# Attention on one NeuronCore: in each half unit the scores for the maximum are sent ahead of the scores for the exponentials

## The chip, the core and the metric

The kernel runs on one core of one Trainium2 chip. A core has five engines that run side by side, each through its own list of instructions in order, and that meet only at semaphores: TensorE (PE in the profile; PEld is its weight load), VectorE (DVE), ScalarE (ACT), GpSimd (POOL) and SyncE (SP, which here only starts DMAs). TensorE writes its results into PSUM, a small memory of 8 banks; VectorE and ScalarE read them there. The metric is the device time of one execution in microseconds (us), the median of the runs.

## What is computed

A "macaron" block on x of 16 x 512 x 128: half a feed-forward layer, an attention layer, half a feed-forward layer, each with a layer norm and a residual. The change touches the attention alone:

```
HEADS, HEAD_DIM = 16, 8
q = (x @ Wq.T + bq).reshape(b, s, HEADS, HEAD_DIM)     # k, v alike
attn = einsum('bqhd,bkhd->bhqk', q, k) / sqrt(HEAD_DIM)
attn = softmax(attn, axis=-1) * head_mask
out = einsum('bhqk,bkhd->bqhd', attn, v) @ Wo.T + bo

x = x + 0.5 * ffn(layernorm(x))      # stage ffn1
x = x + attention(layernorm(x))      # stage attention
x = x + 0.5 * ffn(layernorm(x))      # stage ffn2
```

## The kernel before

The program runs a setup, `ffn1`, `attention` and `ffn2` one after the other. The attention takes 16 batches of 512 rows. The 16 heads are four groups of four, and the 512 positions are four tiles of 128, so that a batch has 16 **units** (a group and a tile), and a unit has two **halves**, of two heads each.

Each score is computed twice. The softmax needs the maximum of each query's scores before the exponentials. So the kernel first computes the scores with the queries on the partitions (`score_max`, L1114; below **max scores**), and VectorE reduces them to the negated maximum (`take_max`, L1372, the reduction on L1379). The maxima of a group are split into two parts on GpSimd (`split_max`), turned on TensorE (`turn_max`), copied on ScalarE (`copy_max`) and packed by DMA into rows of the `q_pack` operand (`pack_max`). The scores that are computed a second time with the keys on the partitions (`score_exp`, L1100; below **exp scores**) then come out with the maximum already taken off, and ScalarE takes their exponentials (`exponential`, L1246, the activation on L1249). The exponentials are multiplied with the values (`times_values`, L1128), accumulated over the four tiles of a group in the bank `p_o`. The max scores run `AHEAD` = 8 units, that is 16 halves, ahead of the exp scores.

A half of either kind of scores is two 32-row by 128-column matmuls with 512 moving columns; the two write the two banks of one **score buffer**. Half 0 of the exp scores uses the array's row strips 0 and 1 and half 1 strips 2 and 3; `HALVES` gives the max scores the other two strips in the same half, so that both kinds can run in the array side by side.

There are three score buffers `p_score` (6 of the 8 banks), and both kinds of scores take them in turn: `order` (L1042 to L1048) lists all halves as they are sent, `place` numbers them, and `score_bank` takes the buffer `place % 3`. `bank_free` (L1055) makes a score wait until the entry three places before it in `order` has been read: by VectorE (semaphore `max_read`) if that is a max score, by ScalarE (`exp_ready`) if it is an exp score.

TensorE's list is written out by hand in `batch` (L1173). Per unit: half 0 sends exp scores, max scores, then one **piece** at most (`pieces`, L1193: a transposition, a projection, all through the one bank `p_x`, whose users wait for each other through `x_bank_filled` and `x_bank_drained`); half 1 sends exp scores, max scores, then `times_values` of the unit before. ScalarE's list is one exponential per half and between them small copies; VectorE's is one reduction per half and between them the statistics of a later layer norm (units 2 and 3), `normalise` (units 2, 6, 10, 14), `residual` (unit 4) and `copy_values` (unit 7). The scores of a group need the packed maxima: before each fourth unit TensorE waits for `max_packed`.

Of the kernel before, what the change touches and what calls it, by code (L numbers as in the profile page):

```python
# [29 lines left out]
NT = S // P  # L30
# [5 lines left out]
NQ = HEADS // QUAD  # L36
# [942 lines left out]
def attention(nc, w, front, src, dst):  # L979
# [6 lines left out]
    MAX_DMA = MAX_PARTS * 16  # L986
    MAX_SPLIT = MAX_PARTS
    inv_sqrt = 1.0 / HD ** 0.5
    with ExitStack() as ctx:
# [25 lines left out]
        max_packed = pair(sem, "max_packed")  # L1015
# [7 lines left out]
        def there(b, n=0):  # L1023

            return not isinstance(b.j, int) or b.k + n < NB
# [16 lines left out]
        order = [("max", 0, n) for n in range(2 * AHEAD)]  # L1042
        for k in range(NB):
            for n in range(PAIRS):
                order.append(("exp", k, n))
                ahead = k * PAIRS + n + 2 * AHEAD
                if ahead < NB * PAIRS:
                    order.append(("max", ahead // PAIRS, ahead % PAIRS))  # L1048
        place = {pair_of_scores: at for at, pair_of_scores in enumerate(order)}

        def score_bank(kind, b, n):

            return p_score[place[kind, b.k, n] % len(p_score)]

        def bank_free(pe, kind, b, n):  # L1055

            at = place[kind, b.k, n] - len(p_score)
            if at >= 0:
                before, k, m = order[at]
                pe.wait_ge({"max": max_read, "exp": exp_ready}[before], k * PAIRS + m + 1)  # L1060
# [36 lines left out]
        def _(pe):  # L1097


            def score_exp(b, u, half):  # L1100

                g, t = divmod(u, NT)
                n = 2 * u + half
                bank_free(pe, "exp", b, n)
                for i in range(2):
                    j = 2 * half + i
                    rows = slice(j * ROWS, (j + 1) * ROWS)
                    last = nc.tensor.matmul(score_bank("exp", b, n)[:, i, :],  # L1108
                                            pack["k"][b.par][rows, g, t * P:(t + 1) * P],
                                            pack["q"][b.par][rows, g, :], start=True, stop=True,  # L1110
                                            tile_position=(j * ROWS, 0))
                last.then_inc(exp_tile, 1)

            def score_max(b, u, half):  # L1114


                g, t = divmod(u, NT)
                n = 2 * u + half
                bank_free(pe, "max", b, n)
                for j in HALVES[half]:  # L1120
                    rows = slice(j * ROWS, (j + 1) * ROWS)
                    last = nc.tensor.matmul(score_bank("max", b, n)[:, j % 2, :],  # L1122
                                            pack["q"][b.par][rows, g, t * P:(t + 1) * P],
                                            pack["k"][b.par][rows, g, :], start=True, stop=True,
                                            tile_position=(j * ROWS, 0))
                last.then_inc(max_tile, 1)

            def times_values(b, u):  # L1128

                g, t = divmod(u, NT)  # L1130
                pe.wait_ge(exp_ready, b.count(PAIRS, 2 * (u + 1)))
                if t == 0:
                    need(pe, o_copied, b.count(NQ, g))
                if u == 0:
                    first_batch = isinstance(b.j, int) and b.k == 0
                    pe.wait_ge(x_bank_drained, FIRST_USES.index("v") + 1 if first_batch
                               else uses(b.step(-1), "v") + 1)
                for h in range(QUAD):
                    last = nc.tensor.matmul(p_o[h * COLS:(h + 1) * COLS, :],  # L1139
                                            values[b.par][:, t, g * QUAD + h, :],  # L1140
                                            exps[(2 * u + h // 2) % len(exps)][:, h % 2, :], start=t == 0, stop=t == NT - 1,
                                            tile_position=(0, h * COLS))
                last.then_inc(pv_done, 1)
# [29 lines left out]
            def batch(b, is_first, is_last):  # L1173
                a, c = b.step(-1), b.step(1)
                for u in range(UNITS):
                    if u % NT == 0:
                        g = u // NT
                        pe.wait_ge(max_packed[g % 2], b.count(MAX_DMA * NQ // 2, MAX_DMA * (g // 2 + 1)))
                    ahead, v = (b, u + AHEAD) if u + AHEAD < UNITS else (c, u + AHEAD - UNITS)
                    if v == 0 and there(ahead):  # L1180
                        pe.wait_ge(packed[ahead.par], ahead.half(PACK_DMA, PACK_DMA))
                    for half in range(2):
                        score_exp(b, u, half)
                        if there(ahead):
                            score_max(ahead, v, half)
                        if half == 0:
                            pieces(b, u, is_first)
                        elif u > 0:
                            times_values(b, u - 1)
                        elif not is_first:  # L1190
                            times_values(a, UNITS - 1)

            def pieces(b, u, is_first):  # L1193
                a, c, e = b.step(-1), b.step(1), b.step(2)
                if u == 1:
                    turn_max(b, 1, uses(b, "m1"))
                if not is_first:
                    if u == 2:
                        turn_o(a, 3, uses(b, "o3"))
                    if u == 3:  # L1200
                        turn_norm(uses(b, "norm"))
                    if u == 4:
                        project_out(uses(b, "out"))
                if u == 5:
                    turn_max(b, 2, uses(b, "m2"))
                if u == 6:
                    turn_o(b, 0, uses(b, "o0"))
                if u == 7 and there(c):
                    front.project_v(pe, p_x, uses(b, "v"))
                if u == 8 and there(e):  # L1210
                    front.turn_x(pe, p_x, e, uses(b, "x"))
                if u == 9:
                    turn_max(b, 3, uses(b, "m3"))
                if u == 10:
                    turn_o(b, 1, uses(b, "o1"))
                if u == 11 and there(e):
                    front.project_qk(pe, p_x, e, w.wq, uses(b, "q"))
                if u == 12 and there(e):
                    front.project_qk(pe, p_x, e, w.wk, uses(b, "k"))
                if u == 13 and there(c):  # L1220
                    turn_max(c, 0, uses(b, "m0"))
                if u == 14:
                    turn_o(b, 2, uses(b, "o2"))
# [292 lines left out]
```

## Time and profile before

| | us |
|---|---|
| time, median of 3 runs | 2008.73 (2007.45 to 2009.02) |
| the profiled execution: its own time | 2005.38 |
| the profiled execution: span from first to last instruction | 2003.2 |
| TensorE busy over the span | 1792.4 (89%) |
| VectorE busy | 1494.7 (75%) |
| ScalarE busy | 1231.5 (61%) |
| GpSimd busy | 891.7 (45%) |

The profile is one execution on the chip. A row of the timeline gives when instructions started, how long they were busy, and in square brackets how long their engine had been idle before and whose work ended that. The attention stage lies between about 602 and 1420 us of the span. Its first scores are sent before 604.26 us, its regular rhythm runs from about 620 us on, and in the last eight units of the last batch no max scores are left to send. TensorE's granted clock is a share of full speed: 1.00 is 2.4 GHz and 0.50 is 1.2 GHz.

### The profile page before, as it was taken

How to read it: one execution, taken by the hardware profiler on the slowest of the kernel's cores; microseconds unless marked ns; L12 is line 12 of the kernel's file. 1: busy time of each engine (PE TensorE's matmuls, PEld its weight loads, DVE VectorE, ACT ScalarE, POOL GpSimd, SP SyncE). 2: the span in 40 equal slices, each digit the busy share in tenths (PEclk: the TensorE clock that was granted, in tenths of full speed). 3: DMA queues.
4: the chain of work that ended last, by engine and by line, in shares of the span. 5: the costliest groups of instructions: out<-in, count | busy, mean ns of one | idle time of the engine just before them, and what ended most of it. 6: DMA issues, size and time to landing. Idle time of an engine off the chain costs nothing. (4 is left out here: it accounts for less than half of the span.)

```text
span 2003.2 us, 30167 instructions
## 1 busy us (share of the span) xinstructions
PE 1792.4 (89%) x9569; PEld 1090.6 (54%) x9600; DVE 1494.7 (75%) x2379; ACT 1231.5 (61%) x1914; POOL 891.7 (45%) x878
## 2 busy tenths in 40 slices
PE   3999999999887888888888888888589999999999
PEld 2777777777662333333333333333267777777777
DVE  4768776877747888888888888888168776877775
ACT  3565555555453777777777777777455556555554
POOL 3665566555661222222222222221145556555655
PEclk9999999999995999999999999999789999999999
DMA  3001000000011111111111111110100000000000
GB/s 95 22 11 32 22 31 10 31 21 19 24 49 45 51 51 51 51 51 51 51 51 51 51 51 51 46 46 13 37 1 33 22 32 11 31 21 30 12 21 11
DMA packets 42269, 69.59 MB, mean 35 GB/s; under 512 B 8508, under 2 KB 10036, under 8 KB 42164
## 3 DMA queue, kind: packets, MB, share of 16 engines
q1 hardware_dynamic: 37360, 66.20, 10.0%
q0 software_dynamic: 4096, 1.08, 0.3%
q8 instruction: 58, 0.95, 0.2%
q10 hardware_dynamic: 708, 0.98, 0.1%
q14 instruction: 47, 0.39, 0.1%
HBM read 28.36 MB, written 12.58 MB: 20 GB/s over the span
## 5 line engine op out<-in xcount | busy, mean ns | idle before, releaser
L762 POOL TENSOR_TENSOR ffn_hid_low<-ffn_hidden,ffn_hid_high 128x512 fp32r<-128x512 f32 x448 | 581.1, 1299 | 457.5 <-ACT ffn_hid_high L674 456.9
L1379 DVE TENSOR_REDUCE attn_neg_max<-attn_p_score 128x2 f32<-128x1024 f32 x512 | 623.5, 1223 | 125.5 <-PE attn_p_score L1122 123.3
L1249 ACT ACTIVATE attn_exps<-attn_p_score 128x1024 f32<-128x1024 f32 x512 | 520.1, 1025 | 219.5 <-PE attn_p_score L1108 217.4
L674 ACT ACTIVATE ffn_hid_high<-ffn_hidden 128x512 fp32r<-128x512 f32 x448 | 281.2, 628 | 257.5 <-DVE ffn_hidden L923 256.0
L665 ACT ACTIVATE ffn_silu<-ffn_p_gate 128x512 f32<-128x512 f32 x448 | 264.3, 590 | 212.8 <-PE ffn_p_gate L518 212.6
L916 DVE TENSOR_TENSOR ffn_gated<-ffn_silu,ffn_p_up 128x512 f32<-128x512 f32 x352 | 240.6, 684 | 181.7 <-PE ffn_p_up L518 118.2
L1122 PE MATMUL attn_p_score<-k_pack,q_pack 32*128 32x512 f32 x1024 | 262.1, 511 | 52.4 <-ACT attn_exps L1249 36.2
L1139 PE MATMUL attn_p_o<-attn_exps,values 128*32 128x512 f32 x2048 | 278.8, 616 | 8.4 <-ACT attn_o_raw L1255 3.4
L1108 PE MATMUL attn_p_score<-q_pack,k_pack 32*128 32x512 f32 x1024 | 253.3, 504 | 1.1 <-DVE attn_neg_max L1379 1.1
L923 DVE TENSOR_TENSOR ffn_hidden<-ffn_gated,ffn_p_spread 128x512 f32<-128x512 f32 x352 | 240.9, 684 | 14.7 <-remote 4.1
L1108 PEld LDWEIGHTS attn_p_score<-q_pack,k_pack 32*128 32x128 f32 x1024 | 95.1, 185 | 266.0 <-issue 235.1
L516 PE MATMUL ffn_p_y<-ffn_hid_high,down_high 128*128 128x512 f32 x448 | 186.5, 416 | 33.6 <-POOL ffn_hid_low L762 32.8
L516 PE MATMUL ffn_p_gate<-ffn_xt_high,gate_high 128*128 128x512 f32 x448 | 189.0, 422 | 0.0
L516 PE MATMUL ffn_p_up<-ffn_xt_high,up_high 128*128 128x512 f32 x448 | 180.9, 404 | 3.1 <-DVE ffn_gated L916 2.9
L1326 POOL DMA_DIRECT2D q_pack<-attn_max_rows x128 | 74.3, 582 | 243.2 <-ACT attn_max_rows L1243 243.2
L518 PE MATMUL ffn_p_gate<-ffn_xt_low,gate_high 128*128 128x512 f32 x448 | 177.6, 397 | 0.0
L518 PE MATMUL ffn_p_up<-ffn_xt_low,up_high 128*128 128x512 f32 x448 | 177.2, 396 | 0.0
L518 PE MATMUL ffn_p_y<-ffn_hid_low,down_high 128*128 128x512 f32 x448 | 177.2, 396 | 0.0
L517 PE MATMUL ffn_p_up<-ffn_xt_high,up_low 128*128 128x512 f32 x448 | 177.1, 395 | 0.0
L517 PE MATMUL ffn_p_gate<-ffn_xt_high,gate_low 128*128 128x512 f32 x448 | 177.0, 395 | 0.0
L517 PE MATMUL ffn_p_y<-ffn_hid_high,down_low 128*128 128x512 f32 x448 | 175.8, 392 | 0.0
L1122 PEld LDWEIGHTS attn_p_score<-k_pack,q_pack 32*128 32x128 f32 x1024 | 96.6, 187 | 107.9 <-ACT attn_exps L1249 91.5
(168 smaller groups left out, 2182.3 us busy)
## 6 DMA issues: line engine op xcount, KB each, us to landing
q_pack<-attn_q_high SPq DMA_DIRECT2D x32, 256.0 KB
k_pack<-attn_k_high SPq DMA_DIRECT2D x32, 256.0 KB
ffn_x_in<-in_x SPq DMA_DIRECT2D x16, 256.0 KB, 2.8
ffn_x_res<-in_x SPq DMA_DIRECT2D x16, 256.0 KB, 3.2
after_ffn<-ffn_x_out SPq DMA_DIRECT2D x16, 256.0 KB, 2.1
attn_x_in<-after_ffn SPq DMA_DIRECT2D x16, 256.0 KB, 2.8
k_pack<-attn_k_low SPq DMA_DIRECT2D x16, 256.0 KB
q_pack<-attn_q_low SPq DMA_DIRECT2D x16, 256.0 KB
```

What stands on the lines that cost most here:

```text
L516: nc.tensor.matmul(out, weights[0], high, start=start, stop=False)
L517: nc.tensor.matmul(out, weights[1], high, start=False, stop=False)
L518: return nc.tensor.matmul(out, weights[0], low, start=False, stop=stop)
L665: nc.scalar.activation(silu[f % 2][0:n, :], p_gate[f % 2][0:n, :], ACT.Silu).then_inc(silu_ready, 1)
L674: nc.scalar.activation(hid_high[s][0:n, :], hidden[s][0:n, :], ACT.Copy).then_inc(high_ready, 1)
L762: nc.gpsimd.tensor_tensor(hid_low[s][0:n, :], hidden[s][0:n, :], hid_high[s][0:n, :].bitcast(F32), ALU.subtract).then_inc(low_ready, 1)
L923: V.tensor_tensor(hidden[slot(b, f)][:], gated[f % 2][:], p_spread[:], ALU.mult).then_inc(weighted_ready, 1)
L1108: last = nc.tensor.matmul(score_bank("exp", b, n)[:, i, :], pack["k"][b.par][rows, g, t * P:(t + 1) * P], pack["q"][b.par][rows, g, :], st ...
L1122: last = nc.tensor.matmul(score_bank("max", b, n)[:, j % 2, :], pack["q"][b.par][rows, g, t * P:(t + 1) * P], pack["k"][b.par][rows, g, :] ...
L1139: last = nc.tensor.matmul(p_o[h * COLS:(h + 1) * COLS, :], values[b.par][:, t, g * QUAD + h, :], exps[(2 * u + h // 2) % len(exps)][:, h % ...
L1249: nc.scalar.activation(exps[n % len(exps)][:], score_bank("exp", b, n)[:], ACT.Exp, scale=inv_sqrt)\
L1379: V.tensor_reduce(neg_max[g % 2][:, j:j + 2, t], score_bank("max", b, n)[:], AX.X, ALU.max, negate=True).then_inc(max_read, 1)
```

## The change

In each half the max scores are sent before the exp scores. `order` is turned in the same way, so that the buffers and the waits follow. With this the entry three places before a max score is the exp score of two halves before, and the entry three places before an exp score is the max score of the half before. Until now it was the exp score of the half before for a max score, and the max score of two halves before for an exp score. The wait for `max_packed`, which stood ahead of a unit's scores, moves into `score_exp`, behind the first max scores of the unit.

```diff
--- before.py
+++ after.py
@@ -1042,10 +1042,10 @@
         order = [("max", 0, n) for n in range(2 * AHEAD)]
         for k in range(NB):
             for n in range(PAIRS):
-                order.append(("exp", k, n))
                 ahead = k * PAIRS + n + 2 * AHEAD
                 if ahead < NB * PAIRS:
                     order.append(("max", ahead // PAIRS, ahead % PAIRS))
+                order.append(("exp", k, n))
         place = {pair_of_scores: at for at, pair_of_scores in enumerate(order)}
 
         def score_bank(kind, b, n):
@@ -1101,6 +1101,8 @@
 
                 g, t = divmod(u, NT)
                 n = 2 * u + half
+                if t == 0 and half == 0:
+                    pe.wait_ge(max_packed[g % 2], b.count(MAX_DMA * NQ // 2, MAX_DMA * (g // 2 + 1)))
                 bank_free(pe, "exp", b, n)
                 for i in range(2):
                     j = 2 * half + i
@@ -1173,16 +1175,13 @@
             def batch(b, is_first, is_last):
                 a, c = b.step(-1), b.step(1)
                 for u in range(UNITS):
-                    if u % NT == 0:
-                        g = u // NT
-                        pe.wait_ge(max_packed[g % 2], b.count(MAX_DMA * NQ // 2, MAX_DMA * (g // 2 + 1)))
                     ahead, v = (b, u + AHEAD) if u + AHEAD < UNITS else (c, u + AHEAD - UNITS)
                     if v == 0 and there(ahead):
                         pe.wait_ge(packed[ahead.par], ahead.half(PACK_DMA, PACK_DMA))
                     for half in range(2):
-                        score_exp(b, u, half)
                         if there(ahead):
                             score_max(ahead, v, half)
+                        score_exp(b, u, half)
                         if half == 0:
                             pieces(b, u, is_first)
                         elif u > 0:
```

TensorE's list in unit 15 of a batch, a unit without a piece, before (rows of L1108 are exp scores, of L1122 max scores; each half is two rows; `attn_p_score0` to `2` are the three buffers, `attn_max_read` is VectorE's semaphore and `attn_exp_ready` ScalarE's; the last row is the first of `times_values`):

```order
L1108 MATMUL attn_p_score0<-q_pack0,k_pack0 128x512 [waits attn_max_read]
L1108 MATMUL attn_p_score0<-q_pack0,k_pack0 128x512
L1122 MATMUL attn_p_score1<-k_pack1,q_pack1 128x512 [waits attn_exp_ready]
L1122 MATMUL attn_p_score1<-k_pack1,q_pack1 128x512
L1108 MATMUL attn_p_score2<-q_pack0,k_pack0 128x512 [waits attn_max_read]
L1108 MATMUL attn_p_score2<-q_pack0,k_pack0 128x512
L1122 MATMUL attn_p_score0<-k_pack1,q_pack1 128x512 [waits attn_exp_ready]
L1122 MATMUL attn_p_score0<-k_pack1,q_pack1 128x512
L1139 MATMUL attn_p_o<-attn_exps4,values0 32x512 [waits attn_exp_ready]
```

The same place now (L1124 are max scores, L1110 exp scores):

```order
L1124 MATMUL attn_p_score0<-k_pack1,q_pack1 128x512 [waits attn_exp_ready]
L1124 MATMUL attn_p_score0<-k_pack1,q_pack1 128x512
L1110 MATMUL attn_p_score1<-q_pack0,k_pack0 128x512 [waits attn_max_read]
L1110 MATMUL attn_p_score1<-q_pack0,k_pack0 128x512
L1124 MATMUL attn_p_score2<-k_pack1,q_pack1 128x512 [waits attn_exp_ready]
L1124 MATMUL attn_p_score2<-k_pack1,q_pack1 128x512
L1110 MATMUL attn_p_score0<-q_pack0,k_pack0 128x512 [waits attn_max_read]
L1110 MATMUL attn_p_score0<-q_pack0,k_pack0 128x512
L1141 MATMUL attn_p_o<-attn_exps4,values0 32x512 [waits attn_exp_ready]
```

The second half's exp scores now stand directly ahead of `times_values` and take the buffer of the first half's max scores, sent three places before; until now the second half's max scores stood there and took the buffer of the first half's exp scores.

Unit 12, which begins a group and has the projection of k (L337 to L339) as its piece, before:

```order
L1108 MATMUL attn_p_score0<-q_pack0,k_pack0 128x512 [waits attn_max_read,attn_max_packed1]
L1108 MATMUL attn_p_score0<-q_pack0,k_pack0 128x512
L1122 MATMUL attn_p_score1<-k_pack1,q_pack1 128x512 [waits attn_exp_ready]
L1122 MATMUL attn_p_score1<-k_pack1,q_pack1 128x512
L337 MATMUL attn_p_x<-attn_xt_high,wk_high 128x512 [waits attn_x_bank_drained,attn_xt_low_ready]
L338 MATMUL attn_p_x<-attn_xt_high,wk_low 128x512
L339 MATMUL attn_p_x<-attn_xt_low,wk_high 128x512
L1108 MATMUL attn_p_score2<-q_pack0,k_pack0 128x512 [waits attn_max_read]
```

and now:

```order
L1124 MATMUL attn_p_score0<-k_pack1,q_pack1 128x512 [waits attn_exp_ready]
L1124 MATMUL attn_p_score0<-k_pack1,q_pack1 128x512
L1110 MATMUL attn_p_score1<-q_pack0,k_pack0 128x512 [waits attn_max_read,attn_max_packed1]
L1110 MATMUL attn_p_score1<-q_pack0,k_pack0 128x512
L337 MATMUL attn_p_x<-attn_xt_high,wk_high 128x512 [waits attn_x_bank_drained,attn_xt_low_ready]
L338 MATMUL attn_p_x<-attn_xt_high,wk_low 128x512
L339 MATMUL attn_p_x<-attn_xt_low,wk_high 128x512
L1124 MATMUL attn_p_score2<-k_pack1,q_pack1 128x512 [waits attn_exp_ready]
```

The wait for the packed maxima (`attn_max_packed1`) now has the unit's first max scores ahead of it. The lists of VectorE, ScalarE, GpSimd and SyncE hold the same operations in the same order as before.

## Rows read from the trace of the kernel before

**Rows 1.** By stretch: length, engines' busy us (count), granted TensorE clock, DMA share, GB/s

```profile
620.00:644.00 24.00, 21.54 (x90) 5.69 (x90) 15.38 (x23) 11.59 (x14) 7.27 (x11) 0.50 0.01 2
644.00:1400.00 756.00, 670.99 (x4592) 260.38 (x4588) 641.78 (x774) 563.38 (x701) 208.11 (x336) 1.00 0.15 47
```

**Rows 2.** Waits between 644 and 1400 us: who <- for whom, us, times, longest

```profile
ACT attn_exps L1249 <- PE attn_p_score L1108: 192.4, 258, 1.9
DVE attn_neg_max L1379 <- PE attn_p_score L1122: 110.2, 322, 1.4
PEld attn_p_score L1122 <- ACT attn_exps L1249: 85.2, 139, 1.0
...
PEld attn_p_score L1108 <- DVE attn_neg_max L1379: 6.5, 32, 0.2
```

**Rows 3.** Timeline of TensorE, units 15 and 0: start, busy, what

```profile
1074.05 1.06 PE L1139 MATMUL attn_p_o<-attn_exps,values 128*32 128x512 f32 x8
1075.04 0.50 PE L1108 MATMUL attn_p_score<-q_pack,k_pack 32*128 32x512 f32 x2
1075.05 0.50 PE L1122 MATMUL attn_p_score<-k_pack,q_pack 32*128 32x512 f32 x2
1075.43 0.50 PE L1108 MATMUL attn_p_score<-q_pack,k_pack 32*128 32x512 f32 x2
1076.66 0.50 PE L1122 MATMUL attn_p_score<-k_pack,q_pack 32*128 32x512 f32 x2 [0.72 <-ACT attn_exps L1249]
1077.09 1.07 PE L1139 MATMUL attn_p_o<-attn_exps,values 128*32 128x512 f32 x8
1078.09 0.50 PE L1108 MATMUL attn_p_score<-q_pack,k_pack 32*128 32x512 f32 x2
```

**Rows 4.** Timeline of ScalarE, the same units

```profile
1075.58 1.94 ACT L1249 ACTIVATE attn_exps<-attn_p_score 128x1024 f32<-128x1024 f32 x2 [0.59 <-PE attn_p_score L1108]
```

**Rows 5.** Timeline of VectorE, the same units

```profile
1074.15 1.23 DVE L1379 TENSOR_REDUCE attn_neg_max<-attn_p_score 128x2 f32<-128x1024 f32 x1 [0.35 <-PE attn_p_score L1122]
...
1077.20 1.23 DVE L1379 TENSOR_REDUCE attn_neg_max<-attn_p_score 128x2 f32<-128x1024 f32 x1 [0.20 <-PE attn_p_score L1122]
```

**Rows 6.** Timeline of TensorE: one piece per batch, in two batches running

```profile
1040.85 1.16 PE L1169 MATMUL attn_p_x<-wo,attn_ot 128*128 128x128 f32 x8
...
1088.54 0.66 PE L1163 MATMUL attn_p_x<-ident,attn_o_norm 128*128 128x128 f32 x4 [0.71 <-DVE attn_o_norm L1393]
...
1091.23 1.16 PE L1169 MATMUL attn_p_x<-wo,attn_ot 128*128 128x128 f32 x8
1092.32 0.50 PE L1108 MATMUL attn_p_score<-q_pack,k_pack 32*128 32x512 f32 x2
```

**Rows 7.** Timeline of VectorE, units 2 to 4

```profile
1086.01 0.86 DVE L262 BATCH_NORM_STATS2 attn_stats<-attn_x_in 128x6 f32<-128x128 f32 x4
1086.78 1.21 DVE L1379 TENSOR_REDUCE attn_neg_max<-attn_p_score 128x2 f32<-128x1024 f32 x1
1087.91 0.25 DVE L1390 RECIPROCAL attn_sums_inv<-attn_p_x 128x16 f32<-128x16 f32 x1
...
1088.40 1.22 DVE L1379 TENSOR_REDUCE attn_neg_max<-attn_p_score 128x2 f32<-128x1024 f32 x1
1089.53 0.15 DVE L269 TENSOR_TENSOR attn_mean_sum<-attn_stats 128x4 f32<-128x4 f32 x1
...
1090.29 2.35 DVE L1379 TENSOR_REDUCE attn_neg_max<-attn_p_score 128x2 f32<-128x1024 f32 x2
...
1094.04 0.68 DVE L1400 TENSOR_TENSOR attn_x_out<-attn_p_x,attn_x_bias 128x512 f32<-128x512 f32 x1
1094.64 2.50 DVE L1379 TENSOR_REDUCE attn_neg_max<-attn_p_score 128x2 f32<-128x1024 f32 x2
```

**Rows 8.** Timeline of TensorE, two units while the granted clock is 0.50

```profile
625.36 0.79 PE L1108 MATMUL attn_p_score<-q_pack,k_pack 32*128 32x512 f32 x2
...
629.86 0.79 PE L1108 MATMUL attn_p_score<-q_pack,k_pack 32*128 32x512 f32 x2
```

## The prediction

> **What bounds the kernel now.** I read the busy time by stretch first. Between 644 and 1400 us, where the attention runs in its regular rhythm, TensorE is busy for 671.0 of 756 us, VectorE for 641.8 and ScalarE for 563.4 [rows 1]. That is 89%, 85% and 75%: nobody is full. The waits come next. ScalarE waits 192.4 us for exp scores, VectorE 110.2 us for max scores, and on TensorE's side 139 weight loads of max scores waited for an exponential, 85.2 us in all, while the exp scores waited only 6.5 us for VectorE's reductions, never over 0.2 us at a time [rows 2]. So the stage is a ring of waits, and the timeline shows which.
>
> Take unit 15, which has no piece. Its first exp scores start at 1075.04 [rows 3]; ScalarE starts on them at 1075.58, 0.54 us later [rows 4]; the second half's max scores, which want that buffer, start at 1076.66, 1.08 us after the exponential's start; `times_values` follows at 1077.09, 0.43 us on; the next unit's exp scores start at 1078.09, 1.00 us later [rows 3]. Sum: 0.54 + 1.08 + 0.43 + 1.00 = 3.05 us, the unit's period. The link through ScalarE's exponential is one of four. VectorE's reductions are a branch beside the ring.
>
> One piece (the output projection) comes back after 1091.23 - 1040.85 = 50.38 us [rows 6]. So a batch takes 50.38 us, against 16 x 3.05 = 48.80. The other 1.58 us are units whose piece waits. The worst that I show: the transposition L1163 waits 0.71 us for VectorE's `normalise` [rows 6].
>
> **The change part by part.** No instruction is added or removed, only TensorE's order and the buffers change. 16 batches x 16 units, less the 8 last units, where no max scores are left, are 248 units, or 15.5 batches, that feel it.
>
> *The new ring.* After `times_values` TensorE sends the first half's max scores, then exp scores, then the second half's max scores, and then exp scores that want the buffer of the first half's max scores. They wait for VectorE's reduction, and `times_values` and everything of the next unit are queued behind them. The links:
> - max scores to the start of their reduction: 0.54 us (1076.66 to 1077.20) [rows 3, 5];
> - start of a reduction to the scores that want its buffer: 1.28 us. The trace shows it once in this unit: reduction at 1074.15, exp scores at 1075.43 [rows 3, 5]. It fits the reduction's 1.23 us;
> - scores to `times_values` 0.43, and that to the next scores 1.00 us, as before.
>
> Sum: 0.54 + 1.28 + 0.43 + 1.00 = **3.25 us** per unit, 0.20 more than now: the exponential's 1.08 is replaced by the reduction's 1.28. 248 x 0.20 = **+49.6 us**.
>
> *The other new waits.* Lay a unit off from its first max scores at 0. The reduction starts at 0.54, the next, queued behind it, at 1.68 (1.14 us from one VectorE start to the next: 1086.78 to 1087.91 is 1.13 [rows 7]), and ends its claim on the buffer at 2.96. The next unit's first exp scores want it at 3.25. 0.29 us of room: no cost. The max scores now want the exponential of two halves before. The second half's exp scores start at 1.82, their exponential at 2.36, the buffer is free at 3.44, and it is wanted by the next unit's second max scores at 3.25 + 0.39 = 3.64. Room 0.20, and a copy of ScalarE between the halves stands behind the exponential, not ahead of it. No cost. The wait for the packed maxima is passed later than before by one pair of scores, and it does not show among the waits now [rows 2]; no cost. SyncE's and GpSimd's DMAs are where they were.
>
> *What VectorE does between its reductions* was beside the ring and is now in it. The statistics (unit 2) take 0.77 us from start to next start (1086.01 to 1086.78), `normalise` 0.49 (1087.91 to 1088.40), the variance steps of unit 3 0.76 (1089.53 to 1090.29), `residual` 0.60 (1094.04 to 1094.64) [rows 7]. I lay units 2 to 5 off in the ring:
> - Unit 2, first max scores at 0. Reductions at 0.54 and, after the statistics, at 2.45 instead of 1.68. `normalise` follows, and VectorE is free at 2.45 + 1.14 + 0.49 = 4.08. Unit 3's max scores are there at 3.25, so that their reduction would have started at 3.79: **+0.29**.
> - Unit 3: reductions at 4.08 and, after the variance steps, at 4.08 + 1.14 + 0.76 = 5.98. Unit 4's first exp scores wait until 5.98 + 1.28 = 7.26, and the projection behind them takes to 7.26 + 0.43 + 1.09 = 8.78 (1091.23 to 1092.32 [rows 6]). Unit 4's second exp scores so start at 8.78; by the ring they would be at 4.08 + 1.28 + 3.25 = 8.61: **+0.17**.
> - Unit 4: the second reduction starts at 9.32, `residual` at 10.46, VectorE is free at 11.06. Unit 5's max scores came at 8.78 + 1.43 = 10.21 and would have been taken at 10.75: **+0.31**.
>
> Sum 0.77 us per batch. The other `normalise` and `copy_values` fall into VectorE's new pause behind the second reduction, from 1.68 + 1.14 = 2.82 to 3.79, so 0.97 us wide, and cost nothing. The pieces' waits that make the 1.58 us of now go: the second max scores are sent at about 0.4 instead of 1.6 us into the unit, so the reduction before `normalise` starts at 1.68 instead of 1.62 + 0.54 = 2.16, and what waited is ready when its turn comes. The pieces themselves (1.09 us at most) fit under 1.82. So a batch has 16 x 3.25 + 0.77 = 52.77 us instead of 50.38, **+2.39**; 15.5 x 2.39 = **+37.0 us**.
>
> At the 0.50 clock the unit is 4.50 us (625.36 to 629.86 [rows 8]), with the same exponential in it, so that the 0.20 holds there too.
>
> Bounds of what the trace doesn't show: with no extra at all in a batch, 15.5 x (16 x 3.25 - 50.38) = +25.1; with the 1.58 us of now staying and nothing new, +49.6; with 0.77 on top, +61.5. I take 37.0, since each wait was laid off by itself.
>
> What a reader costs is also in the notes. By the Trainium skill (Perfetto Trace Analysis, Optimizing Scalar/DVE Operations) an access to PSUM costs VectorE about 125 ns beyond the elements and ScalarE about 51 ns, and with the clocks of Trainium Kernel Development and Optimization, NeuronCore Architecture (0.96 and 1.2 GHz) 1024 elements give an estimate of 1.19 and 0.90 us, 0.29 apart. The trace shows the two from start to next user 1.28 and 1.08, 0.20 apart. By the page's 0.29 the first term would be 71 us instead of 49.6, and the time about 2067; I go by the trace.
>
> **Level.** The profiled execution took 2005.38 us with a span of 2003.2. The new span: 2003.2 + 37.0 = 2040.2. On the median of 2008.73: **2045.7 us**.
>
> **The rivals.**
> *Faster: VectorE is fed sooner.* VectorE is the busier of the two readers and its 110.2 us of waiting are for the very scores that are now sent first [rows 2]. If its earlier start shortened the ring, the 1.58 us per batch would be won and nothing paid: -15.5 x 1.58 = -24.5, so 1984. It decides if the new link through the reduction is no longer than the old one, that is if max scores at TensorE are released within 0.54 + 1.08 = 1.62 us; the row gives 1.82. Against it: the first max scores of a unit cannot be sent before `times_values`, which stands behind the wait for the last ones, so VectorE only trades a pause in mid-unit for one of 0.97 us at its end.
> *No change.* The gain on the pieces offsets the ring: with 1.58 us gone and nothing new, this needs a ring only 0.10 us longer, so a release 1.18 us after the reduction's start. The row has 1.28 and the reduction alone is busy for 1.23. About 2009.
> *The clock falls.* TensorE stands still within each unit from the second max scores to the exp scores, 0.5 + 0.4 to 1.82, 0.9 us instead of 0.72 now [rows 3]. At 0.50 a unit takes 4.50 against 3.05 [rows 3, 8], so each unit there costs 1.45 us. A stage wholly at 0.50 would take 240 x 1.45 = 348 us more, about 2390; a later rise at the start by five units 7 us. For it: the clock was at 0.50 from 620 to 644 us although TensorE was busy 21.5 of 24 us [rows 1]. Against it: it then stayed at 1.00 through 756 us with a standstill of 0.72 us in each unit.
> The Trainium skill (Perfetto Trace Analysis, Matmul Optimizations) says that TensorE's power scales with its use and that matmuls should be sent back to back; by it this rival is the one to fear, while the trace so far shows the full clock with pauses.
>
> **How the numbers follow.** The forecast, a longer ring with between +25 and +61 us, holds 0.88; faster by the first rival 0.04; no change 0.04; the clock 0.04. The range of 2032 to 2064 runs from the lower bound (2033.8) to a little over 2058, the case of the old waits staying, and most of the way to the upper one (2070). A measurement of this kernel can tell about 0.2% from no change, 4 us. Faster by more than that 0.04, within it 0.04, slower 0.92.
>
> **What would show it.** The output projection comes back after 52.8 us instead of 50.38. In unit 15 the second half's exp scores start 1.82 us after the first max scores and wait for VectorE, the max scores wait for nobody, and TensorE's waits for exponentials (85.2 us) turn into waits for reductions of some 0.9 us per unit, over 200 us in all. ScalarE and VectorE still wait, VectorE now ahead of each unit's first reduction. Units 3, 4 and 5 are longer than 3.25 us by 0.29, 0.17 and 0.31, and the others are not. Wrong if units of 3.05 us are left, if L1163 still waits 0.7 us, or if the granted clock is below 1.00 after 650 us.

## The result and the profile after

| | before | changed |
|---|---|---|
| median, us | 2008.09 (4 runs, 2006.14 to 2009.02) | 2059.41 (4 runs, 2058.55 to 2059.99) |
| profiled execution: its time / its span, us | 2005.38 / 2003.2 | 2059.99 / 2057.8 |
| mean granted TensorE clock | 0.978 | 0.969 |

The ratio is 1.0257, with a 95% interval of 1.0239 to 1.0274: the change makes the kernel slower by 51.3 us.

The ring is read first. The timeline of TensorE in the changed kernel, the last unit of one batch and the first of the next, answers to [rows 3] (L1124 max scores, L1110 exp scores, L1141 `times_values`):

```profile
1110.85 0.49 PE L1124 MATMUL attn_p_score<-k_pack,q_pack 32*128 32x512 f32 x2
1110.85 0.50 PE L1110 MATMUL attn_p_score<-q_pack,k_pack 32*128 32x512 f32 x2
1111.19 0.40 PE L1124 MATMUL attn_p_score<-k_pack,q_pack 32*128 32x512 f32 x2
1112.66 0.50 PE L1110 MATMUL attn_p_score<-q_pack,k_pack 32*128 32x512 f32 x2 [1.07 <-DVE attn_neg_max L1378]
1113.09 1.06 PE L1141 MATMUL attn_p_o<-attn_exps,values 128*32 128x512 f32 x8
1114.09 0.50 PE L1124 MATMUL attn_p_score<-k_pack,q_pack 32*128 32x512 f32 x2
```

and VectorE's row of the same unit, two reductions one behind the other:

```profile
1111.38 2.36 DVE L1378 TENSOR_REDUCE attn_neg_max<-attn_p_score 128x2 f32<-128x1024 f32 x2 [0.40 <-PE attn_p_score L1124]
```

The max scores of the first half start at 1110.85, their reduction at 1111.38 (0.53 later), the exp scores that want the buffer at 1112.66 (1.28 later), `times_values` at 1113.09 (0.43 later), the next unit at 1114.09 (1.00 later). Sum 3.24; forecast 0.54 + 1.28 + 0.43 + 1.00 = 3.25, before 3.05. The max scores of the second half go out at 1111.19, right behind the first ones, and then TensorE stands still for 1.07 us, on VectorE.

The waits in the same stage, between 644 and 1456 us, answer to [rows 2]:

```profile
ACT attn_exps L1248 <- PE attn_p_score L1110: 226.4, 426, 1.7
...
DVE attn_neg_max L1378 <- PE attn_p_score L1124: 169.8, 235, 2.3
PEld attn_p_score L1110 <- DVE attn_neg_max L1378: 149.4, 220, 1.5
PE attn_p_score L1110 <- DVE attn_neg_max L1378: 79.0, 154, 1.1
```

TensorE's weight loads waited 85.2 us for exponentials before; now they wait 149.4 us for reductions. VectorE, whose scores are now sent first, waits longer, not less: 169.8 instead of 110.2 us. Its waits are fewer (235 instead of 322); in the unit above the one wait stands before the first reduction (0.40 us), and the second reduction follows without one.

The output projection, once per batch, answers to [rows 6]:

```profile
1071.62 1.16 PE L1171 MATMUL attn_p_x<-wo,attn_ot 128*128 128x128 f32 x8
...
1128.35 1.16 PE L1171 MATMUL attn_p_x<-wo,attn_ot 128*128 128x128 f32 x8
...
1181.47 1.16 PE L1171 MATMUL attn_p_x<-wo,attn_ot 128*128 128x128 f32 x8
```

A batch now takes 1181.47 - 1128.35 = 53.12 us, and so do the batches around it, against 50.38. The one before it took 56.73. The view by stretch, with the granted clock before the DMA share, tells why, and answers to [rows 1] (length, busy us of TensorE, its weight loads, VectorE, ScalarE and GpSimd, clock, DMA share, GB/s):

```profile
602.00:662.00 60.00, 47.51 (x198) 16.51 (x198) 44.02 (x50) 23.29 (x27) 9.70 (x18) 0.57 0.12 41
702.00:707.00 5.00, 5.00 (x32) 2.00 (x24) 2.73 (x5) 2.74 (x4) 1.20 (x2) 0.68 0.10 37
752.00:762.00 10.00, 9.47 (x53) 3.24 (x49) 6.99 (x8) 5.76 (x7) 2.98 (x6) 0.72 0.18 57
1072.00:1090.00 18.00, 17.18 (x92) 7.28 (x91) 12.05 (x14) 9.58 (x11) 4.38 (x9) 0.72 0.09 31
1090.00:1456.00 366.00, 318.63 (x2104) 121.18 (x2102) 289.70 (x346) 266.28 (x321) 91.42 (x150) 1.00 0.13 42
```

The clock, at 1.00 throughout the rhythm before, falls to 0.50 three times, for 3 to 10 us each (about 702 to 705, 756 to 763 and 1077 to 1087 us); below these are the **dips**, and at the start of the stage it rises at about 654 us instead of about 644.

The span is 54.6 us longer. By the projection's periods:
- 15.5 batches x (53.12 - 50.38) = **42.5 us**, the ring and what is in it;
- the three batches with a dip took 54.25, 55.48 and 56.73 us, together **7.1 us** more than three of 53.12;
- the first projection comes 85.11 us after the first transposition of the maxima instead of 78.91, 6.2 us more, of which the ring in 20 units explains 3.4 (20/16 x 2.74): the later rise takes about **2.8 us**;
- that first transposition itself is 1.85 us later than before. The rest is 0.3 us.

That the later rise makes up the whole of the 2.8 us is not shown.

### The profile page after: what moved, and what is told of

It is laid out like the page before. It is cut to its first block and busy times, and to the rows that moved or that the text cites. A ratio compares the mean times of both kernels' runs of the same rounds, so it can differ in the third digit from the quotient of the medians.

```text
span 2057.8 us, 30213 instructions
## 1 busy us (share of the span) xinstructions
PE 1836.1 (89%) x9600; PEld 1105.1 (54%) x9600; DVE 1487.6 (72%) x2379; ACT 1249.6 (61%) x1914; POOL 892.1 (43%) x878
## 3 DMA queue, kind: packets, MB, share of 16 engines
q0 software_dynamic: 4096, 1.08, 0.3%
## 5 line engine op out<-in xcount | busy, mean ns | idle before, releaser
L1378 DVE TENSOR_REDUCE attn_neg_max<-attn_p_score 128x2 f32<-128x1024 f32 x512 | 612.0, 1222 | 184.3 <-PE attn_p_score L1124 180.7
L1110 PE MATMUL attn_p_score<-q_pack,k_pack 32*128 32x512 f32 x1024 | 261.2, 510 | 85.7 <-DVE attn_neg_max L1378 83.5
L1141 PE MATMUL attn_p_o<-attn_exps,values 128*32 128x512 f32 x2048 | 283.2, 625 | 6.9 <-ACT attn_o_raw L1254 5.9
L1124 PE MATMUL attn_p_score<-k_pack,q_pack 32*128 32x512 f32 x1024 | 254.9, 509 | 8.4 <-DVE attn_neg_max L1378 5.1
L1124 PEld LDWEIGHTS attn_p_score<-k_pack,q_pack 32*128 32x128 f32 x1024 | 97.7, 190 | 268.3 <-issue 211.5
L1110 PEld LDWEIGHTS attn_p_score<-q_pack,k_pack 32*128 32x128 f32 x1024 | 97.1, 186 | 175.9 <-DVE attn_neg_max L1378 157.2
```

Of the source, the lines that this page charges most:

```text
L1110: last = nc.tensor.matmul(score_bank("exp", b, n)[:, i, :], pack["k"][b.par][rows, g, t * P:(t + 1) * P], pack["q"][b.par][rows, g, :], st ...
L1141: last = nc.tensor.matmul(p_o[h * COLS:(h + 1) * COLS, :], values[b.par][:, t, g * QUAD + h, :], exps[(2 * u + h // 2) % len(exps)][:, h % ...
L1378: V.tensor_reduce(neg_max[g % 2][:, j:j + 2, t], score_bank("max", b, n)[:], AX.X, ALU.max, negate=True).then_inc(max_read, 1)
```

## The experiments

The theory: the ring of waits through the buffer that the first scores after `times_values` fill sets the unit's length. The rivals: VectorE or ScalarE bounds the stage in either order; what counts is only which kind of scores stands ahead of `times_values`; the moved wait for the packed maxima; the clock. All ratios are to the kernel before in the same comparison, and the batch is the period of the output projection at the full clock.

### Either reader made shorter, in both orders

```diff
-  V.tensor_reduce(neg_max[...], score_bank("max", b, n)[:], AX.X, ...)
+  V.tensor_reduce(neg_max[...], score_bank("max", b, n)[:, :, 0:416], AX.X, ...)
```

> The changed kernel, with each maximum taken over 416 of its 512 keys; the other keys are left out of the maximum (the softmax is the same with any offset near it). A reduction has 832 instead of 1024 elements and should be some 0.20 us shorter. Theory (the ring goes through VectorE's reduction): a unit goes from 3.25 to 3.05 us, 248 units give 50 us back, and if the dips of TensorE's clock inside the attention come from the longer standstills they go too: 2059 becomes about 2000 to 2010. Rival (VectorE is beside the ring and the loss is the clock or something of TensorE's own): a unit stays at 3.25 us and the time at about 2059.

> The kernel before, with the same shorter maximum over 416 of 512 keys. Theory: the reduction is a branch beside the ring, a unit stays at 3.05 us; only the pieces' waits for VectorE shrink, by at most 1.58 us per batch, so between 1984 and 2008. Rival (VectorE bounds both orders): 40 to 50 us faster here too, about 1960.

```diff
-  nc.scalar.activation(exps[...][:], score_bank("exp", b, n)[:], ACT.Exp, scale=inv_sqrt)
+  cols = slice(0, S if b.k == 0 else 416)
+  nc.scalar.activation(exps[...][:, :, cols], score_bank("exp", b, n)[:, :, cols], ACT.Exp, scale=inv_sqrt)
```

> The changed kernel, with the exponentials of 416 of 512 queries in all batches but the first; the exponentials of the other queries are left out there. An exponential should be some 0.16 us shorter. Theory: ScalarE is now beside the ring, a unit stays at 3.25 us and the time within 6 us of 2059; the cost of 0.25 us in unit 13, where the multiplication with the values waits for a copy of ScalarE, goes: up to 4 us. Rival (ScalarE still in the ring): 35 us faster, about 2024.

> The kernel before, with the same shorter exponentials (416 of 512 queries, the others are left out from the second batch on). Theory: the exponential is in the ring, 232 units lose 0.16 us each, 37 us faster, about 1971. Rival (VectorE bounds): no change, about 2008.

The groups between 800 and 1400 us (busy, mean ns of one) of the changed kernel with the short reduction, and then of the kernel before with the short exponential, show the sizes:

```profile
L1378 DVE TENSOR_REDUCE attn_neg_max<-attn_p_score 128x2 f32<-128x832 f32 x384 | 388.2, 1024 | 164.7 <-PE attn_p_score L1124 163.4 <-POOL attn_max_parts L1318 0.6
```

```profile
L1250 ACT ACTIVATE attn_exps<-attn_p_score 128x832 f32<-128x832 f32 x399 | 341.2, 864 | 190.8 <-PE attn_p_score L1108 188.6
```

A reduction is 0.20 us shorter (1.22 to 1.02), an exponential 0.16 us (1.02 to 0.86).

| | median, us | ratio to before (95%) | batch, us |
|---|---|---|---|
| changed order, short reduction | 2001.81 | 0.9973 (0.9963 to 0.9982) | 50.23 |
| old order, short reduction | 1994.51 | 0.9941 (0.9921 to 0.9961) | 49.64 |
| changed order, short exponential | 2052.19 | 1.0224 (1.0179 to 1.0269) | 52.83 |
| old order, short exponential | 1974.24 | 0.9840 (0.9813 to 0.9867) | 48.54 |

0.20 us off the reduction is worth 2.89 us per batch in the changed order (53.12 to 50.23) and 0.74 in the old one; 0.16 us off the exponential 1.83 in the old order and 0.29 in the changed one, where `times_values` no longer waits for ScalarE's copy in unit 13 (below). So the reader in the ring is VectorE after the change and ScalarE before it. With the short reduction the unit of the changed kernel reads 3.05 us from max scores to max scores, with its standstill at 0.88 instead of 1.07:

```profile
1021.54 0.50 PE L1124 MATMUL attn_p_score<-k_pack,q_pack 32*128 32x512 f32 x2
...
1023.16 0.50 PE L1110 MATMUL attn_p_score<-q_pack,k_pack 32*128 32x512 f32 x2 [0.88 <-DVE attn_neg_max L1378]
...
1024.59 0.50 PE L1124 MATMUL attn_p_score<-k_pack,q_pack 32*128 32x512 f32 x2
```

These four rule out that one and the same reader bounds the stage in both orders.

### The order turned in one half only

```diff
+  maxima = [("max", ahead // PAIRS, ahead % PAIRS)] if ahead < NB * PAIRS else []
+  order.extend(maxima + [("exp", k, n)] if n % 2 == H else [("exp", k, n)] + maxima)
...
+  if half != H: score_exp(b, u, half)
   if there(ahead): score_max(ahead, v, half)
+  if half == H: score_exp(b, u, half)
```

> The changed kernel, but the max scores go first in half 0 only; in half 1 the exp scores go first, as before the change, so that max scores stand ahead of the multiplication with the values. Theory: they take the buffer of the max scores of half 0, so the ring goes through the reduction: 3.25 us per unit, about 2050 to 2060. Rival (what counts is that exp scores stand ahead of the values): 3.05 us per unit, about 2008.

> The reverse: the max scores go first in half 1 only. The exp scores of half 1, ahead of the multiplication with the values, now take the buffer of the exp scores of half 0. Theory: the ring goes through the exponential, 3.05 us per unit, and the time is near 2008 (2000 to 2020). Rival (exp scores ahead of the values cost the time, whichever buffer they take): about 2059.

Max scores first in half 0 only: 2092.29 us, ratio 1.0415 (1.0391 to 1.0440), batch 53.42 at the full clock. Max scores first in half 1 only: 2012.02 us, ratio 1.0029 (1.0019 to 1.0039), batch 50.82. In the first the scores ahead of `times_values` are max scores, as before the change, and the ring is the longer one all the same, since their buffer comes from a reduction; in the second they are exp scores, as after it, and the ring is the short one:

```profile
1028.67 0.50 PE L1109 MATMUL attn_p_score<-q_pack,k_pack 32*128 32x512 f32 x2
1028.68 0.73 PE L1123 MATMUL attn_p_score<-k_pack,q_pack 32*128 32x512 f32 x4
1030.29 0.50 PE L1109 MATMUL attn_p_score<-q_pack,k_pack 32*128 32x512 f32 x2 [0.88 <-ACT attn_exps L1250]
1030.72 1.07 PE L1140 MATMUL attn_p_o<-attn_exps,values 128*32 128x512 f32 x8
1031.71 0.50 PE L1109 MATMUL attn_p_score<-q_pack,k_pack 32*128 32x512 f32 x2
```

(max scores first in half 1, TensorE; L1109 are exp scores: 3.04 us, with the wait for ScalarE.) In these four orders what counts is the kind of scores sent first after `times_values`. Where the second kernel's other 0.44 us per batch (50.82 against 50.38) come from was not followed up. The first of the two was 32 us above the top of its forecast, 2050 to 2060: its clock in the stage was 0.92, as its stretch from 644 us on shows:

```profile
644.00:1480.00 836.00, 725.79 (x4545) 272.62 (x4547) 638.10 (x769) 560.57 (x694) 206.71 (x333) 0.92 0.13 42
```

### The moved wait alone

```diff
   for u in range(UNITS):
+      if u % NT == 0: pe.wait_ge(max_packed[g % 2], ...)      # back in its old place
       ...
   def score_exp(b, u, half):
-      if t == 0 and half == 0: pe.wait_ge(max_packed[g % 2], ...)
```

> The changed kernel with the wait for the packed maxima back in its old place, ahead of the unit's first max scores. Theory: the packed maxima are there long before either place; the time is that of the changed kernel, 2059, within 3 us. Rival (the moved wait is part of the loss): more than 4 us faster.

2057.83 us, ratio 1.0259 (1.0240 to 1.0279), batch 53.02 against 53.12. The wait's place is worth 0.1 us a batch at most; the loss is the order's.

### The same ring length in the old order

```diff
   need(act, pv_done, ...)
+  nc.scalar.activation(spare[:, n % len(exps), :], w.ident[0:32, :], ACT.Copy)
   nc.scalar.activation(exps[n % len(exps)][:], ...)
```

> The kernel before with a small activation (a copy of 32x128) on ScalarE behind the wait for the exp scores, ahead of each exponential, so that the link through ScalarE is longer by that copy, 0.15 to 0.25 us, and the ring about as long as in the changed kernel, with the old order. Theory of the clock (TensorE's longer standstill in each unit makes the granted clock fall now and then): stretches at 0.50 inside the attention appear here too, and the time is that of the ring (248 x 0.2 = 50 us) and some 10 us more, 2055 to 2075. Rival (the dips belong to the changed order): the clock holds 1.00 from its rise to the end of the attention, and the time is 2045 to 2058.

2052.57 us, ratio 1.0221 (1.0201 to 1.0241), batch 52.79. TensorE's unit:

```profile
1050.36 0.50 PE L1109 MATMUL attn_p_score<-q_pack,k_pack 32*128 32x512 f32 x2
...
1052.17 0.50 PE L1123 MATMUL attn_p_score<-k_pack,q_pack 32*128 32x512 f32 x2 [0.91 <-ACT attn_exps L1251]
...
1053.60 0.50 PE L1109 MATMUL attn_p_score<-q_pack,k_pack 32*128 32x512 f32 x2
```

3.24 us, the length of the changed kernel's unit, made in the old order by 0.2 us in ScalarE's link. It costs 2.41 us per batch; the change costs 2.74. Its clock held 1.00 from the rise to the end of the rhythm (a stretch of 786 us has 0.99, its first microseconds below). So a longer ring with a standstill of 0.91 us does not by itself bring the dips.

### ScalarE's copy ahead of the multiplication in unit 13

The changed kernel's unit 13 is 3.50 us, not 3.25. TensorE and, below, ScalarE:

```profile
1105.92 0.50 PE L1110 MATMUL attn_p_score<-q_pack,k_pack 32*128 32x512 f32 x2 [0.26 <-DVE attn_neg_max L1378]
1106.60 1.06 PE L1141 MATMUL attn_p_o<-attn_exps,values 128*32 128x512 f32 x8 [0.18 <-ACT attn_o_raw L1254]
```

```profile
1104.14 0.68 ACT L360 ACTIVATE attn_k_full<-attn_p_x,bk 128x512 f32<-128x512 f32 x1
1104.94 1.02 ACT L1248 ACTIVATE attn_exps<-attn_p_score 128x1024 f32<-128x1024 f32 x1
1105.86 0.59 ACT L1254 ACTIVATE attn_o_raw<-attn_p_o 128x512 f32<-128x512 f32 x1
```

`times_values` starts 0.68 us after the scores instead of 0.43, since the copy of the last group's sums (L1254) stands behind an exponential whose scores had waited for VectorE. The copy moved up by half a unit:

```diff
-  if now == (13, 0):
+  if now == (12, 1):          # ahead of the copy of k
       copy_o(b, 2, uses(b, "o0") + 1)
```

> The changed kernel with ScalarE's copy of the third group's output sums moved ahead of the copy of k (half 1 of unit 12 instead of half 0 of unit 13). Theory: the 0.25 us per batch that the multiplication in unit 13 waits for that copy go, 15 x 0.25 = 4 us faster than 2059, if the later copy of k does not make the next transposition late by more than its room. Rival: the copy of k comes 0.5 us later, TensorE waits for it in unit 13, and the time is the same or worse.

The batch goes from 53.12 to 52.86 us, by the 0.25 us that the wait was long. (A transposition now waits up to 0.7 us for the later copy of k, the rival's mechanism, but within the time in which the exp scores behind it would have waited for VectorE.) The median did not follow: 2059.37 us, ratio 1.0258 (1.0230 to 1.0285), with single runs from 2044.16 to 2060.33. The profiled execution is the shortest (2044.16 us, mean granted clock 0.978, with one short dip); the other four took 2058.88 to 2060.33 at 0.966 or 0.967. So the clock differs between executions of one kernel, here along with some 15 us.

### The multiplication moved between the two scores of half 1

```diff
   score_exp(b, u, half)
+  if half == 1: times_values(b, u - 1)
   if there(ahead): score_max(ahead, v, half)
-  ... times_values(b, u - 1)
```

> The kernel before with the multiplication with the values of half 1 between that half's exp scores and its max scores, instead of behind both. Theory: the max scores wait 1.08 us for the exponential's end, and the multiplication takes 1.00 us of that; TensorE's ring is gone and a unit is bounded by what VectorE (2 x 1.14 us and its other work, 2.3 us per unit plus 4.6 us per batch) or TensorE does: 2.4 to 2.8 us per unit instead of 3.15, so 90 to 180 us faster, 1830 to 1920. Rival (the ring is not what bounds): no change, about 2008.

> The changed kernel with the multiplication with the values between the max scores and the exp scores of half 1. Theory: the wait for the reduction is covered in the same way, and both orders come out within 1% of each other, 1830 to 1930. Rival: the order itself costs its 50 us whatever covers the wait, so that it stays 2% to 3% slower than the one above.

Both forecasts were far off. The first took 2267.15 us (its runs from 2230.03 to 2277.62, so that even the shortest is 11% above the kernel before), the second 2411.45 us, ratio 1.2021 (1.1974 to 1.2067). Three things failed. First, the wait was not covered but handed on. TensorE in the first of them, at the full clock:

```profile
893.05 0.70 PE L1122 MATMUL attn_p_score<-k_pack,q_pack 32*128 32x512 f32 x4
893.39 0.40 PE L1108 MATMUL attn_p_score<-q_pack,k_pack 32*128 32x512 f32 x2
894.88 0.50 PE L1108 MATMUL attn_p_score<-q_pack,k_pack 32*128 32x512 f32 x2 [1.09 <-DVE attn_neg_max L1380]
895.31 1.07 PE L1139 MATMUL attn_p_o<-attn_exps,values 128*32 128x512 f32 x8
896.30 0.79 PE L1122 MATMUL attn_p_score<-k_pack,q_pack 32*128 32x512 f32 x4
```

The unit is 3.25 us again, now in the old order. A unit has four scores and the ring three buffers, so the scores right behind `times_values` and the scores right ahead of the next one always share a buffer. Here those behind it are max scores, and the link is the reduction. I had followed only the pair that waited before the edit.

Second, the pieces. In the second kernel exp scores stand behind `times_values`, so by that rule its unit should be 3.05 us, and it is not. TensorE, at a granted clock of 1.00:

```profile
1178.33 1.07 PE L1141 MATMUL attn_p_o<-attn_exps,values 128*32 128x512 f32 x8
...
1181.52 0.27 PE L1150 MATMUL attn_p_x<-ident,attn_max_parts 128*32 128x128 f32 x1 [1.30 <-ACT attn_xt L351]
...
1182.92 1.06 PE L1141 MATMUL attn_p_o<-attn_exps,values 128*32 128x512 f32 x8 [0.71 <-ACT attn_o_raw L1255]
...
1185.77 0.63 PE L1158 MATMUL attn_p_x<-ident,attn_o_raw 128*128 128x128 f32 x4 [1.12 <-ACT attn_max_rows L1243]
...
1186.76 1.07 PE L1141 MATMUL attn_p_o<-attn_exps,values 128*32 128x512 f32 x8
```

These two units take 4.59 and 3.84 us. TensorE waits for ScalarE's small copies, which stand behind exponentials in ScalarE's list, first in the piece and then in `times_values`: waits that the ring leaves out.

Third, the clock: TensorE's stretches show 0.78 and, for the second kernel, 0.70:

```profile
644.00:1500.00 856.00, 681.91 (x3817) 253.38 (x3819) 524.96 (x656) 484.64 (x587) 179.14 (x286) 0.78 0.11 36
```

```profile
644.00:1600.00 956.00, 775.38 (x3893) 277.89 (x3889) 551.00 (x667) 474.52 (x600) 183.11 (x291) 0.70 0.10 34
```

### The multiplication split over the two halves

```diff
+  split = u in (0, 1, 5, 9, 13, 15)
+  if (u > 0 or not is_first) and (split or half == 1):
+      times_values(*of, (2 * half, 2 * half + 1) if split else (0, 1, 2, 3))
```

> The kernel before, with the multiplication with the values split over the two halves (heads 0 and 1 in half 0, heads 2 and 3 in half 1) in units 0, 1, 5, 9, 13 and 15, the ones without a piece or with the short one; nothing is left out. The theory that came out of the runs so far: with three buffers and four scores per unit, the scores right behind the multiplication are read and their buffer is wanted by the scores right ahead of the next one, so that a unit takes 0.54 us, the read, 0.43 us and the whole multiplication, wherever it stands. Split, each of the two rings holds 0.5 us of it: 2.55 us and 2.55 us plus the piece (0.20), instead of 3.05. ScalarE's copies in units 9 and 13 (three of 0.2 to 0.6 us beside two exponentials) leave less there. Expected: 0.3 to 0.5 us in each of units 0, 1, 5 and 15 and little in the others, 1.2 to 2.4 us per batch, so 19 to 38 us faster if the clock holds: 1970 to 1990. Rival: the clock falls in the attention as it did when the multiplication was moved between the scores, and the time is above 2050; the granted clock tells the two apart.

2144.87 us, ratio 1.0682 (1.0659 to 1.0705). The granted clock between 800 and 1380 us was 0.96, but the larger part is in the order: the shortest period of the output projection in it is 56.94 us, against 50.38. Units 15 and 0 of TensorE's timeline:

```profile
1029.43 0.50 PE L1108 MATMUL attn_p_score<-q_pack,k_pack 32*128 32x512 f32 x2
...
1029.87 1.05 PE L1139 MATMUL attn_p_o<-attn_exps,values 128*32 128x512 f32 x4
1030.85 0.50 PE L1108 MATMUL attn_p_score<-q_pack,k_pack 32*128 32x512 f32 x2
...
1032.45 0.50 PE L1108 MATMUL attn_p_score<-q_pack,k_pack 32*128 32x512 f32 x2
```

Half a multiplication (x4, two heads) holds TensorE from 1029.87 to 1030.85, 0.98 us; the whole one (x8, four heads) takes 1.00 us. So four heads take hardly longer than two, and splitting nearly doubles their time: unit 15 is 3.02 us against 3.05, with next to nothing won. And in units 5, 9 and 13 half the multiplication stands ahead of the unit's second exp scores and waits for ScalarE's copy of the sums, 1.57 us at 1023.76 (and 1.63 us for an exponential in unit 1, at 1037.63):

```profile
1023.76 1.05 PE L1139 MATMUL attn_p_o<-attn_exps,values 128*32 128x512 f32 x4 [1.57 <-ACT attn_o_raw L1256]
```

No order that I ran with all the work in it beats the kernel before.

## Why the prediction was right, and where it was off

- **The ring.** 0.54 + 1.28 + 0.43 + 1.00 was forecast, 0.53 + 1.28 + 0.43 + 1.00 measured. Waits for reductions of over 200 us were forecast too, and TensorE's weight loads show 149.4: the full 0.9 us and more stands only in units without a piece (1.07 in unit 15), while a piece fills part of it (0.30 us are left at 1122.41). That the reduction takes the exponential's place is shown by the two shortened readers in both orders, and that the order and no other part of the edit does it by the two half-turned orders and the wait put back.
- **Units 3, 4 and 5.** Forecast +0.29, +0.17 and +0.31 us; from one unit's second exp scores to the next (1122.41, 1125.93, 1129.45 and 1132.98 us) they measure +0.27, +0.27 and +0.28.
- **The pieces' waits.** Forecast: they go. The transposition that waited 0.71 us for `normalise` (L1163, now L1165) waits for nothing at 1124.80. Mostly right: the transposition behind `residual` still waits 0.18 instead of 0.43 us, and two kinds of pieces wait for ScalarE's copies, up to 0.4 us (0.2 before) and 0.3 us (none before). The exp scores behind those would have waited anyway.
- **The batch.** Forecast 52.77, measured 53.12. The step that failed is the one by which a copy of ScalarE between the halves costs nothing. In unit 13 the multiplication waits 0.25 us for one, and the run with the copy moved up took just that back (52.86). I had laid off the buffers' waits and left out the wait of `times_values` for `o_copied`. Of the other 0.10 us, 0.05 are in units 3 to 5, and 0.05 are not traced. In all 15.5 x 0.35 = 5.4 us of the time.
- **The clock.** I gave its fall a chance of 0.04 and took it as a case by itself. It came together with the forecast, and with it one of my own signs of being wrong, a clock below 1.00 after 650 us: dips for 7.1 us, a later rise for 2.8 us. With 37.0 + 5.4 + 9.9 = 52.3 us the measured 51.3 is accounted for. The forecast of 2045.7 was 13.7 us too low, within its range of 2032 to 2064. That it stayed inside is in part luck: the upper end had been drawn for the case that the old waits stay, and they went; the forecast has nothing for the 9.9 us of the clock. The argument against the fall, that 756 us with a standstill of 0.72 us per unit had kept the clock, did not cover a standstill of 1.07, which I had put at 0.9 from the lengths of the matmuls.
- **The price by the Trainium skill.** Perfetto Trace Analysis, Optimizing Scalar/DVE Operations, gave an estimate of 0.29 us between the two readers, and of 71 us for the ring; the trace shows 1.28 - 1.08 = 0.20, which makes 49.6 us. The trace decides.

What stays open is why the clock dips. Within the rhythm of the profiled executions it never fell in the kernel before, with the short reduction or the short exponential in the old order, with the short reduction in the changed order, with max scores first in half 1, nor with the longer exponential. It fell in the changed kernel and in its variants with the wait put back, with the early copy and with the short exponential, more with max scores first in half 0 and with the multiplication split, and most with the multiplication between the scores. Between 700 and 1290 us the longest single standstill of TensorE is 0.73 to 0.92 us in each of the six kernels where it held, and 1.09 us or more in all eight where it fell. The Trainium skill (Perfetto Trace Analysis, Matmul Optimizations) says that TensorE's power follows its use. From kernel to kernel the runs agree with that, but the place of the dips does not. In the changed kernel all three begin 5.4 to 5.8 us behind the start of an output projection, in unit 5 of a batch, in which TensorE had waited (at the third) only 0.18 and 0.34 us, and none begins in units 15 and 0, with their standstills of 1.07 us. By stretch, ahead of the third dip, in it, and in the units 15 and 0 that follow:

```profile
1073.00:1077.00 4.00, 3.47 (x25) 1.18 (x25) 3.76 (x4) 2.75 (x4) 1.81 (x4) 1.00 0.26 85
1077.50:1078.00 0.50, 0.50 (x4) 0.00 (x0) 0.00 (x0) 0.46 (x2) 0.00 (x0) 0.50 0.24 90
1110.00:1114.00 4.00, 2.93 (x24) 0.72 (x17) 3.31 (x5) 2.81 (x3) 1.27 (x2) 1.00 0.00 0
```

TensorE was busier just before the fall (3.47 of 4 us) than where the clock held (2.93 of 4). So long standstills and dips go together, but that the one makes the other is not shown: no run here varied the standstill alone.

## What to carry to other kernels

Where buffers are taken in turn, count them against the entries of one period of the engine that fills them: the longest piece of work in its list (here 1.00 us of multiplication) is in a ring with the read of whatever is sent right behind it, so put behind it what is read fastest. That holds only while nothing else is longer: the multiplication between the scores of the changed order had the short reader behind it and was the slowest kernel of all, on waits for ScalarE's copies and on the clock. Sending an idle engine's work first does not feed it, if the place in the list where that work may start is itself behind a wait. After such a reordering, lay off every wait of each step against the new times, the small copies of the third engine too, and watch the granted clock.

## What the runs showed of the hardware

- Two of the four heads' multiplications, placed in different 32-column strips, take 0.98 us, and all four 1.00: here the third and fourth strip cost 0.02 us together.
- The granted clock fell to 0.50 within a stage of which TensorE was busy for 87% by the profile in a stretch without a dip (changed kernel, 318.6 of 366 us), and it kept 1.00 with 88% (old order with the longer exponential, 509.6 of 580 us between 800 and 1380) and 89% [rows 1]. The busy share does not tell them apart. The dips and the later rise go with 9.9 us of the changed kernel; how much of the 403 us of the slowest kernel is due to its mean clock of 0.70 is open.
